# Two of a chunk's sixteen products with B on GpSimd, their decay in PSUM

## The reference

```python
x, z = jnp.split(h @ in_proj_w, 2, axis=-1)
x = silu(causal_depthwise_conv(x, conv_w, conv_b))
A = -jnp.exp(A_log)
xp = x @ x_proj_w                      # 64 columns for delta, 16 for B, 16 for C
delta = softplus(xp[..., :64] @ dt_proj_w + dt_proj_b)
dA  = exp(delta[..., None] * A)        # the decay
dBu = delta[..., None] * B[:, :, None, :] * x[..., None]
h_t = dA_t * h_{t-1} + dBu_t           # scan over the 1024 tokens
y_t = sum_n(h_t[:, n] * C_t[n]) + x * D_param
out = (y * silu(z)) @ out_proj_w
```

## Time and profile before

| | |
|---|---|
| Median of 3 runs | 3248.03 us (3246.77 to 3251.04) |
| The profiled execution's own time | 3248.44 us |
| Its span, first to last instruction | 3246.6 us |
| Busy, share of the span | PE 84%, DVE 82%, POOL 67%, ACT 53% |
| Granted TensorE clock, mean | 0.892 of full speed |

### The profile page before, as it was taken

One profiled execution on the slowest core, in us unless ns is written; L12 is line 12 of the kernel. 1 busy time (PEld: TensorE's weight loads), 2 busy tenths in 40 slices (PEclk: granted clock), 3 DMA queues, 4 the chain that ended last, 5 costly groups with the idle time before them and its releaser, 6 DMA issues. The chain is left out here.

```text
span 3246.6 us, 31734 instructions
## 1 busy us (share of the span) xinstructions
PE 2717.0 (84%) x10349; PEld 1394.6 (43%) x10349; DVE 2650.3 (82%) x2498; ACT 1705.8 (53%) x2427; POOL 2175.2 (67%) x1219
## 2 busy tenths in 40 slices
PE   2999999776878878978978978878867659999998
PEld 1565556452324424424414424424422125655555
DVE  6777777407999999999999999999999946777775
ACT  3444444335665756666666666666654513444443
POOL 4566666306787877877777787777787735555652
PEclk9999999987888978979978978978966669999999
DMA  3011111108678687686776776767767720110100
GB/s 103 20 49 40 49 49 39 43 13 195 155 174 198 158 194 179 163 199 167 175 189 172 179 191 165 187 167 176 189 164 187 188 75 14 33 33 26 32 26 20
DMA packets 173304, 387.82 MB, mean 119 GB/s; under 512 B 22502, under 2 KB 90150, under 8 KB 172902
## 3 DMA queue, kind: packets, MB, share of 16 engines
q1 hardware_dynamic: 155382, 367.06, 45.5%
q10 hardware_dynamic: 17776, 18.94, 2.0%
HBM read 308.26 MB, written 52.49 MB: 111 GB/s over the span
## 5 line engine op out<-in xcount | busy, mean ns | idle before, releaser
L971 POOL TENSOR_TENSOR mix_scan<-mix_scan,mix_bc 128x1024 f32<-128x1024 f32 x512 | 1204.6, 2355 | 396.0 <-DVE mix_scan L1126 395.3
L1126 DVE TENSOR_TENSOR_SCAN mix_scan<-mix_decay,mix_ps_du 128x1024 f32<-128x1024 f32 x512 | 1170.0, 2285 | 63.1 <-ACT mix_decay L1072 20.6
L1138 DVE TENSOR_TENSOR mix_ps_du<-mix_ps_du,mix_bc 128x1024 f32<-128x1024 f32 x512 | 618.2, 1207 | 134.6 <-PE mix_ps_du L1239 134.0
L1239 PE MATMUL mix_ps_du<-mix_stack,mix_sel 96*128 96x512 bf16 x1024 | 366.6, 446 | 376.5 <-DVE mix_scan L1126 355.0
L716 PE MATMUL ffn_ps_gate_up<-ffn_w_gate_up,ffn_xT 128*128 128x512 f32 (+1 forms) x1536 | 656.5, 564 | 14.3 <-DVE ffn_h L480 14.0
L1072 ACT ACTIVATE mix_decay<-mix_decay,mix_a_neg 128x1024 f32<-128x1024 f32 x512 | 573.7, 1141 | 114.2 <-DMA mix_decay<-delta_rows 113.2
L755 PE MATMUL ffn_ps_down<-ffn_w_down,ffn_hT 128*128 128x256 f32 (+1 forms) x1536 | 382.4, 391 | 12.1 <-ACT ffn_hT L639 12.1
L716 PEld LDWEIGHTS ffn_ps_gate_up<-ffn_w_gate_up,ffn_xT 128*128 128x128 f32 x1536 | 273.1, 191 | 259.6 <-issue 218.3
L1239 PEld LDWEIGHTS mix_ps_du<-mix_stack,mix_sel 96*128 96x128 bf16 x1024 | 78.6, 103 | 685.6 <-DVE mix_scan L1126 554.9
L612 POOL TENSOR_TENSOR ffn_h_scaled<-ffn_h,ffn_h_recip 128x1408 f32<-128x1408 f32 x64 | 188.3, 2943 | 235.4 <-ACT ffn_h_recip L689 235.4
L1221 PE MATMUL mix_ps_y<-mix_scan,mix_red 128*32 128x512 f32 x2048 | 340.3, 747 | 4.8 <-POOL mix_scan L971 4.8
(11 more groups left out here) (136 smaller groups left out, 3712.8 us busy)
## 6 DMA issues: line engine op xcount, KB each, us to landing
mix_decay<-delta_rows SPq DMA_DIRECT2D x512, 512.0 KB, 7.1
mix_stack<-mix_parts SPq DMA_DIRECT2D x384, 64.0 KB, 2.0
delta_rows<-mix_delta SPq DMA_DIRECT2D x32, 512.0 KB, 3.1
ffn_x<-_attn_hidden_states_dram SPq DMA_DIRECT2D x32, 256.0 KB, 3.1
after_ffn<-ffn_y SPq DMA_DIRECT2D x32, 256.0 KB, 3.2
normed_ffn<-ffn_y_normed SPq DMA_DIRECT2D x32, 256.0 KB, 3.2
mix_x_tokens<-normed_ffn SPq DMA_DIRECT2D x32, 256.0 KB, 12.1
mix_x_residual<-after_ffn ACTq DMA_DIRECT2D x32, 256.0 KB, 4.0
```

Source lines behind the costliest of these rows:

```text
L971: G.tensor_tensor(wt, wt, bc[:, r % 2, 1, :], ALU.mult).then_inc(hc_done, 1)
L1126: V.tensor_tensor_scan(w[:, slot % RING, :], da[:, slot % SPREADS, :], ps_du[:, slot % 2, :], 0.0, ALU.mult, ALU.add).then_inc(scan_done, 1)
L1138: V.tensor_tensor(ps_du[:, slot % 2, :], ps_du[:, slot % 2, :], bc[:, r % 2, 0, :], ALU.mult)\
L1239: ins = M(ps_du[:, slot % 2, h * 512:(h + 1) * 512], const.sel[0:SEL, i, :], stack[:, c % 2, q, h * 512:(h + 1) * 512], start=True, stop=True)
```

## The change

Slots 3 and 15 of every chunk (`POOL_SLOTS`) get their product with B from GpSimd instead of VectorE.

- GpSimd's product takes delta*u from SBUF: SP stores rows 96 to 127 of a chunk's delta*u in DRAM (`keep_du`), and `spread_du` copies the slot's 8 rows to the tile `du_rows`, of which there is one, four slots ahead.
- GpSimd multiplies `du_rows` by B into the slot's buffer of `w`, two slots ahead, before the product with C of that earlier slot.
- The matmuls of `replicate` fall away for these slots. The PSUM buffer that is free takes the decay instead, and the exponential of these slots stands one slot ahead, not two, and waits until the scan two slots earlier has left the buffer. The scan reads decay from PSUM and product from `w`, in place.
- The second part of the cut of delta*u (`REST1`) also waits until the rows are in DRAM.
- The selection matrix for B and C moves into unused rows of the tile of `w_dt`.

```diff
+POOL_SLOTS = (3, 15)
+POOL_ROWS = 96
+SPREAD_DU = 4
...
+            def keep_du(b, c):
+                sy.wait_ge(du_done, chunk(b, c))
+                sy.dma_start(du_dram[c % 2, :, :], du[POOL_ROWS:P, :]).then_inc(du_kept, 16)
+
+            def spread_du(r, R, slot):
+                c, s = divmod(slot, SLOTS)
+                sy.wait_ge(du_kept, 16 * chunk(R, c))
+                if by_pool(R, slot) > 1:
+                    sy.wait_ge(pool_dbu, by_pool(R, slot) - 1)
+                row = 32 * (s % 4) + 8 * (s // 4) - POOL_ROWS
+                sy.dma_start(du_rows[:, :],
+                             du_dram[c % 2, row:row + NCH, :].unsqueeze(0).to_broadcast([NST, NCH, L]))\
+                  .then_inc(du_spread[(by_pool(R, slot) - 1) % 2], 16)
...
+                        if s - LATER[c] == SCALE + 1:
+                            keep_du(b, cc)
...
                     if core(rr, full):
                         spread_delta(rr, R2, at)
+                    rr, R2, at = ahead(r, R, slot, SPREAD_DU)
+                    if core(rr, full) and at % SLOTS in POOL_SLOTS:
+                        spread_du(rr, R2, at)
...
+                    if core(r, full) and s + 2 in POOL_SLOTS:
+                        n = by_pool(R, slot + 2)
+                        pool.wait_ge(du_spread[(n - 1) % 2], 16 * ((n + 1) // 2))
...
+                        G.tensor_tensor(w[:, (slot + 2) % RING, :], du_rows[:, :], bc[:, r % 2, 0, :], ALU.mult).then_inc(pool_dbu, 1)
                     if core(r, full):
                         pool.wait_ge(scan_done, R * 64 + (slot + 1))
...
                         if s - LATER[c] == REST1:
                             pool.wait_ge(cast1, n)
+                            pool.wait_ge(du_kept, 16 * n)
...
+            def decay(r, R, at, c, s):
...
+                if s in POOL_SLOTS:
+                    act.wait_ge(scan_done, R * 64 + (at - 1))
+                    to = ps_du[:, at % 2, :]
+                A.activation(to, da[:, at % SPREADS, :], ACT.Exp, scale=const.aneg[:, qi:qi + 1]).then_inc(exp_done, 1)
...
+                    for by in (LEAD - 1, LEAD):
+                        rr, R2, at = ahead(r, R, slot, by)
                         c2, s2 = divmod(at, SLOTS)
...
+                        if core(rr, full) and by == (LEAD - 1 if s2 in POOL_SLOTS else LEAD):
+                            decay(rr, R2, at, c2, s2)
...
+                if slot % SLOTS in POOL_SLOTS:
+                    dve.wait_ge(pool_dbu, by_pool(R, slot))
+                    state = w[:, slot % RING, :]
+                    V.tensor_tensor_scan(state, ps_du[:, slot % 2, :], state, 0.0, ALU.mult, ALU.add)\
+                     .then_inc(scan_done, 1)
...
             def replicate(r, R, slot):
 
                 c, s = divmod(slot, SLOTS)
+                if s in POOL_SLOTS:
+                    return
```

More of the change, by code:

```diff
@@ L211, in _ @@
         G.memset(const.minus[:, :], -1.0)
-        G.memset(const.zeros[:, :, :], 0.0)
-        G.memset(const.sel_bc[:, :, :], 0.0)
+        then(G.memset(const.zeros[:, :, :], 0.0))
+        then(G.memset(const.sel_bc[:, :, :], 0.0))
         G.memset(const.red[:, :, :, :], 0.0)
@@ L866, in mixer @@
         y_made, yg_done = S("y_made"), S("gate_done")
+        du_kept, du_spread, pool_dbu = S("delta_u_kept"), [S(f"delta_u_spread{k}") for k in range(2)], S("pool_dbu")
         res_in, out_stored = [S(f"res_in{k}") for k in range(4)], [S(f"out_stored{k}") for k in range(4)]
@@ L907, in chunk, with by_pool @@
             return b * CHUNKS + (c + 1)
+        def by_pool(R, slot):
+            c, s = divmod(slot, SLOTS)
+            return (R * CHUNKS + c) * len(POOL_SLOTS) + sum(t <= s for t in POOL_SLOTS)
         @block.sync
@@ L967, in program @@
                     c, s = divmod(slot, SLOTS)
+                    if core(r, full) and s + 2 in POOL_SLOTS:
+                        n = by_pool(R, slot + 2)
+                        pool.wait_ge(du_spread[(n - 1) % 2], 16 * ((n + 1) // 2))
+                        if slot + 2 < SLOTS:
+                            pool.wait_ge(taken["B"], (R + 1) * 4)
+                        if slot + 2 >= RING or r > 0:
+                            pool.wait_ge(y_made, R * 16 + (slot + 2 - RING) // 4 + 1)
+                        G.tensor_tensor(w[:, (slot + 2) % RING, :], du_rows[:, :], bc[:, r % 2, 0, :], ALU.mult).then_inc(pool_dbu, 1)
                     if core(r, full):
@@ L1122, in scan @@
                 dve.wait_ge(exp_done, n)
-                dve.wait_ge(dbu_done, n)
-                if slot >= 8 or r > 0:
-                    dve.wait_ge(y_made, R * 16 + (slot - 8) // 4 + 1)
-                V.tensor_tensor_scan(w[:, slot % RING, :], da[:, slot % SPREADS, :], ps_du[:, slot % 2, :], 0.0,
-                                     ALU.mult, ALU.add).then_inc(scan_done, 1)
+                if slot % SLOTS in POOL_SLOTS:
[3 more added lines that the diff above has]
+                     .then_inc(scan_done, 1)
+                else:
+                    dve.wait_ge(dbu_done, n - by_pool(R, slot))
+                    if slot >= 8 or r > 0:
+                        dve.wait_ge(y_made, R * 16 + (slot - 8) // 4 + 1)
+                    V.tensor_tensor_scan(w[:, slot % RING, :], da[:, slot % SPREADS, :], ps_du[:, slot % 2, :], 0.0,
+                                         ALU.mult, ALU.add).then_inc(scan_done, 1)
             def program(r, R, full):
@@ L1132, in program @@
                     c, s = divmod(slot, SLOTS)
-                    if core(r, full):
-                        n = R * 64 + (slot + 1)
-                        dve.wait_ge(rep_du, n)
+                    if core(r, full) and s not in POOL_SLOTS:
+                        dve.wait_ge(rep_du, R * 64 + (slot + 1) - by_pool(R, slot))
                         if slot == 0:
@@ L1187, in make @@
                     pe.wait_ge(taken["X"], b * 4 + 4)
-                    ins = M(job, const.sel_bc[RANK:RANK + 2 * NST, which, :],
+                    ins = M(job, const.sel_bc[:, which, :],
                             xp[RANK:RANK + 2 * NST, par, h * 512:(h + 1) * 512], start=True, stop=True)
```

22 lines of the change are left out of this document (11 added, 11 removed).

## The result

The changed kernel takes 3344.39 us (median of 4 runs, 3340.29 to 3358.46) against 3247.41 for the one before on the same chip: ratio 1.0304, 95% interval 1.0273 to 1.0335. The forecast was 3286 us, at most 3335. The direction was right, and the loss is two and a half times the one forecast: 97 us instead of 38. The profiled execution has a span of 3341.9 us, 95.3 more than before.

The account below looks back on a forecast made before the run. VectorE was taken to set the mixer's pace. Per batch -0.3 - 4.8 + 14.1 - 3.8 = +5.2 us, 1.3 a chunk; +40 over 31 chunks, -2.4 in the last: 3248.4 + 38 = 3286 us, range 3200 to 3335.

Parts of the forecast that it names:

- the products: VectorE's products with B in 2 of 16 slots, 32 chunks: 64 of 1.207 us taken away, 77.2 us at most won.
- the 0 between bounds: Scan and decay through PSUM: taken as no change in length, bounds 0.2 us less to 0.2 us more for each.
- Slot 15's wait for delta*u: VectorE's scan waits for GpSimd's product, whose spread lands late in the burst: 3.2, 2.4, 3.5, 5.0 us, +14.1 a batch.
- Old waits: Earlier VectorE waits swallowed by new ones: 0.6 and 1.1 us at slot 3, 3.8 at the second chunk's start, per batch.
- the sentence that TensorE and ScalarE work on during the new wait: During slot 15's wait both catch up, removing waits of 2.52 and 1.29 us at the second chunk's start: -3.8 a batch.
- Delta*u for slot 3: Next chunk's spread, queued behind others, and GpSimd's product from it: ready 0.8 us before slot 3's scan, counted as 0.
- the decay in slot 3: ScalarE's decay behind slot 2's jobs: -1.2, +1.4, -1.1, +0.6 us in the four chunks, -0.3 a batch.
- GpSimd as the bound: Rival: the single delta*u tile makes slot 3's product late, each chunk losing some 3 us more: 3380 us, chance 0.08.
- Decays stay late: Rival: slot 15's delta*u lands in time, but decays at slots 3 and 15 stay late: 3209 us, chance 0.20.

Follow-up runs that it names:

- the first experiment: Changed kernel with only slot 15's delta*u spread moved, issued seven slots ahead instead of four, before the burst: 3246.95 us, ratio 0.9991 to the kernel before.

## Why the prediction was wrong

**Right.** VectorE sets the pace, and the products are worth 77.0 us (forecast 77.2). The scan from PSUM costs 2.286 us, its decay 1.11, so the 0 between bounds holds. Slot 15's wait for delta*u is 120.5 us in 31 chunks (forecast 109); but for the very first chunk (5.5 us), first chunks wait for nothing in slot 3. Old waits worth about 42 us are gone (the batch's 0.6, 1.1 and 3.8 make 44): in the window VectorE's other idle time went from 96 to 53. So the sentence that TensorE and ScalarE work on during the new wait holds for the waits it names. Delta*u for slot 3 was held to be in time by 0.8 us. In the changed kernel it was, but only since everything behind slot 15 came later; with both late steps mended VectorE waited 48 us for GpSimd there.

**The step that failed** is the decay in slot 3: the time at which TensorE has done slot 2's job. The prediction took it from the earlier trace rows and moved it ahead by what TensorE no longer does, 0.6, 2.4 and 1.0 us. All other steps of TensorE kept the length that they had in that trace, where the clock over slots 0 to 2 was 1.00 in the second and fourth chunk of the third batch. In the changed kernel it was 0.71 and 0.62. In the fourth chunk, counted from slot 0's scan (1432.13; before it was 1394.5, three slots of 3.5 ahead of slot 3's in the earlier trace rows), the take of the job ended at 15.2 us (1447.37) instead of 11.1 (1405.57): 4.2 later, where I had 1.0 sooner. That is 5.2 us off, and the four steps shown above are 5.4 us longer. Over all chunks slot 3 waited 84.5 us, 5.5 of them for GpSimd, instead of the forecast 50. Where the clock stayed at 1.00, slot 3 waited no more than forecast, but for 3.31 us against 3.2. The same step is missing behind slot 15: I put the slots there at nothing, and with slot 15 alone TensorE is late in slots 2 to 4 by 33 us instead of 7.

The miss is 57 us of the profiled execution's span: slot 3 +34, slot 15 +11, the window's edges +6, VectorE's busy time, which fell by 73.6 instead of 77.2, +4, and old waits +2. The single changes split it in another way. For slot 3 alone the forecast's steps give -2 us, and it measured -1 (3248.32 against 3249.02): its waits for the decay, 47 us, come near the forecast 50, as long ones in fourth chunks stand beside none in third chunks. For slot 15 alone they give 14.1 - 4.8 - 3.8 = 5.5 us a batch, 1.4 a chunk, 43 in 31 chunks and 1.2 won in the last, so 41, and it measured 81. The 40 us between are 13 of longer waits for the landing and about 26 of TensorE's lateness in the slots behind.

**Shown:** that the late delta*u costs 97 us with the late decay and 145 without it (3328 to 3183); that slot 3's wait follows the granted clock, with and without a wait at slot 15; and that less work for TensorE in slots 0 to 3 brings 59 and 63 us, 11 and 9 of them ahead of the first scan. **Open:** what sets the clock there. In the second and third chunks it was lower in the changed kernel than with delta*u early, which differ by the place of one transfer; in the fourth chunks it was not. TensorE's idle time ahead of the chunk doesn't decide it either. It is 3.75 or 3.76 us in all seven fourth chunks of the changed kernel, whose clock then ranges from 0.58 to 1.00, and 1.99 us in all seven with slot 3 alone, from 0.66 to 1.00.

**The rivals.** GpSimd as the bound did not happen: it idled 159 us ahead of its products with C. "Decays stay late" has its mechanism in the first experiment, and there it is 3247, not 3209: the same jobs, 67 us of waits at slot 3 where I had about 50, 26 at slot 15 where I had 4 for a batch, 32, and 17 for GpSimd.

## What to carry to other kernels

A step's length on TensorE, read from a trace, holds only at the clock of that trace. Before such a time goes into a sum, read the granted clock of the same stretch in several batches, and ask what the sum would be at the other level: here four steps took 11.6 us instead of 6.2. A step that stands early and ahead of others hides such stretches; moved one slot later and behind the jobs, the decay no longer did. So the slack given up is worth as much thought as the time won. Two late steps are not worth the sum of their costs: measure the square of both, and mend the first of the chain first (here the decay's order was worth 64 us with delta*u early, 16 with it late). A transfer is given its lead in time by its place in the queue: moving one spread ahead of a burst of overdue ones brought 97 us, and nothing else changed.

## What the hardware did unasked

TensorE, busy 4.00 of 4.00 us in three windows on end (1436 to 1448), kept a granted clock of 0.50; before, in the same place and with the same work, it was at 1.00. It had idled 3.75 us ahead of the chunk, against 1.99. But in the changed kernel's fifth batch it idled 3.76 us in the same place, and the clock over slots 0 to 2 was 1.00. Activity as the profile counts it did not by itself bring the clock back.

A VectorE scan with both inputs in SBUF beside GpSimd's products takes up to 4.38 us instead of 2.29, and GpSimd's up to 4.36 instead of 2.36. With one input in PSUM the scan never took over 2.29 us.
